# GpSimd's order in a cross attention step: six table entries ahead of the delta's factor

## What is computed

```python
delta = ctx @ Wo.T + bo                       # after softmax attention over ctx_2048, 16 heads
delta = rs * delta
mu, var = mean(delta), mean((delta - mu) ** 2)
delta = (delta - mu) / sqrt(var + EPS_LN) * ln_gamma + ln_beta
x = x + delta
xf = layernorm(x)
scores = softmax(xf @ gate_weight.T)          # 64 experts in 8 groups, best 3 groups, best 6 experts
slot = expert * 192 + position of the token in its expert
```

## Time and profile before

| | us |
|---|---|
| median of three timed runs | 1599.75 (1599.74 to 1600.75) |
| the profiled execution, its own time | 1597.56 |
| its span, first to last instruction | 1595.9 |
| TensorE busy | 1486.6 (93%) |
| VectorE busy | 1139.3 (71%) |
| ScalarE busy | 897.5 (56%) |
| GpSimd busy | 772.4 (48%) |
| cross attention, steps 0 to 15 and what follows the loop | about 325 to 655 |

### The profile page before, as it was taken

The page is one execution under the profiler, slowest core; times in us unless marked ns, Lnnn a source line. Parts: engine busy times, 40 slices in busy tenths (PEclk is TensorE's granted clock), DMA queues, the critical chain, the costliest instruction groups (busy, mean ns, idle before and its releaser), DMA issues.

```text
span 1595.9 us, 30498 instructions
## 1 busy us (share of the span) xinstructions
PE 1486.6 (93%) x10360; PEld 1232.2 (77%) x10360; DVE 1139.3 (71%) x2054; ACT 897.5 (56%) x1769; POOL 772.4 (48%) x957
## 2 busy tenths in 40 slices
PE   6999998999999865499999999999999999999997
PEld 4788886778888754388888888888888888777866
DVE  5677757557888787577777777777777777565656
ACT  4565666644544331187777777777777778412111
POOL 2122234233365556265565555565555564437543
PEclk9999999999999976599999999999999999999999
DMA  6012212222211110598777787777887775437553
GB/s 205 7 55 85 62 54 91 95 71 74 75 66 41 41 54 34 202 365 294 270 266 259 275 289 264 267 267 263 277 289 263 268 262 200 137 119 225 178 177 119
DMA packets 109217, 275.48 MB, mean 173 GB/s; under 512 B 16592, under 2 KB 16592, under 8 KB 109136
## 3 DMA queue, kind: packets, MB, share of 16 engines
q1 hardware_dynamic: 91392, 223.53, 41.0%
q0 software_dynamic: 15360, 50.34, 9.8%
q10 hardware_dynamic: 2384, 0.53, 0.2%
HBM read 232.41 MB, written 41.94 MB: 172 GB/s over the span
## 4 chain that ended last, share of the span: by engine, by line
PE 55%; DVE 2%; DMA 1%; issue 0%; POOL 0%; ACT 0%; SPq 0%; DVEq 0%; POOLq 0%
PE e_gu L2386 18%; PE e_gu L2388 9%; PE e_dn_rest L2414 5%; PE e_tr L49 3%; PE e_dn_main L41 3%; PE e_dn_main L43 3%; PE e_dn_main L42 3%; PE h_gt L41 1%; PE h_gt L43 1%; PE h_gt L42 1%; PE h_up L43 1%; PE h_up L41 1%; PE h_up L42 1%; PE h_dn L41 1%; DVE h_acc L2663 1%; PE h_dn L42 1%
## 5 line engine op out<-in xcount | busy, mean ns | idle before, releaser
L2149 POOL TENSOR_TENSOR e_hid<-e_h_raw,e_hid 128x128 fp32r<-128x128 f32 (+1 forms) x192 | 165.6, 863 | 221.3 <-ACT e_hid L2214 221.3
L2386 PE MATMUL e_gu<-e_xT_hi_lo,e_wg 128*128 128x384 f32 (+1 forms) x768 | 231.5, 357 | 1.6 <-issue 1.6
L2386 PE MATMUL e_gu<-e_xT_hi_lo,e_wu 128*128 128x384 f32 (+1 forms) x768 | 230.4, 355 | 0.0
L2388 PE MATMUL e_gu<-e_xT_hi_lo,e_wu 128*128 128x192 f32 (+1 forms) x768 | 193.3, 252 | 0.0
L2388 PE MATMUL e_gu<-e_xT_hi_lo,e_wg 128*128 128x192 f32 (+1 forms) x768 | 193.1, 251 | 0.0
L2157 POOL TENSOR_TENSOR e_wd<-e_raw_d,e_wd 96x512 fp32r<-96x512 f32 x64 | 131.6, 2056 | 35.8 <-ACT e_wd L2199 35.8
L2386 PEld LDWEIGHTS e_gu<-e_xT_hi_lo,e_wg 128*128 128x128 f32 (+1 forms) x768 | 138.0, 180 | 6.8 <-issue 2.6
L2292 DVE TENSOR_TENSOR e_total<-e_gu,e_low 128x384 f32<-128x384 f32 (+1 forms) x192 | 105.5, 549 | 51.5 <-ACT e_low L2209 51.5
L2388 PEld LDWEIGHTS e_gu<-e_xT_hi_lo,e_wg 128*128 128x128 f32 (+1 forms) x768 | 139.8, 182 | 1.4
L2386 PEld LDWEIGHTS e_gu<-e_xT_hi_lo,e_wu 128*128 128x128 f32 (+1 forms) x768 | 137.9, 180 | 3.8
L2388 PEld LDWEIGHTS e_gu<-e_xT_hi_lo,e_wu 128*128 128x128 f32 (+1 forms) x768 | 139.7, 182 | 0.0
(11 more groups left out here) (341 smaller groups left out, 4049.3 us busy)
## 6 DMA issues: line engine op xcount, KB each, us to landing
e_raw_g<-in_L_ffn_Wg_dram SPq DMA_DIRECT2D x64, 704.0 KB, 4.3
e_raw_u<-in_L_ffn_Wu_dram SPq DMA_DIRECT2D x64, 704.0 KB, 5.7
e_raw_d<-in_L_ffn_Wd_dram SPq DMA_DIRECT2D x64, 512.0 KB, 5.9
y_dram<-e_y_main SPq DMA_DIRECT2D x64, 256.0 KB, 6.2
e_raw_d<-in_L_ffn_Wd_dram SPq DMA_DIRECT2D x64, 192.0 KB, 6.4
y_dram<-e_y_rest SPq DMA_DIRECT2D x64, 128.0 KB, 7.0
s_xr<-in_x_dram SPq DMA_DIRECT2D x16, 256.0 KB, 3.8
x_dram<-s_x SPq DMA_DIRECT2D x16, 256.0 KB, 2.5
```

The costliest lines, as they stand in the source:

```text
L2149: pool.tensor_tensor(hid[b][1][0:n, c, :], h_raw[g.odd][b][0:n, c, 0:P], hid[b][0][0:n, c, :].bitcast(F32), ALU.subtract).then_inc(s_hl, 1)
L2386: pe.matmul(bank[0:n, 0:2 * CAP], w[b][0][:, k, m:m + n], xT[:, :, k, toks], start=k == 0, stop=False)
L2388: ins = pe.matmul(bank[0:n, 0:CAP], w[b][1][:, k, m:m + n], xT[:, 0, k, toks], start=False, stop=k == KC - 1)
```

## The change

In GpSimd's loop the call of `delta_factor(t - 1)` moves behind the table entries. What stands ahead of both, and what follows the loop, is the same; no instruction is added or taken out on any engine.

```diff
                 for m in cross_fresh(t + 1):
                     inv_std(m)
-                if t >= 1:
-                    delta_factor(t - 1)
                 for g in range(NG - 3):
                     for i in range(CROSS_GROUPS[g][1] - CROSS_GROUPS[g][0]):
                         if group_steps(g)[1] + i == t:
                             table_entries(g, i)
+                if t >= 1:
+                    delta_factor(t - 1)
             final_rstd(BATCH - 2)
```

## The result

The median of four timed runs is 1610.97 us (1609.23 to 1613.59), against 1599.74 us of the kernel before on the same chip: a ratio of 1.0065, 95% interval 1.0051 to 1.0079. The change costs 11.2 us. In a second comparison the same kernel came out at 1609.96 us against 1602.59, ratio 1.0054 (1.0035 to 1.0073). So 0.54 to 0.65%; the medians differ by 11.2 and 7.4 us, and the two intervals together reach from 0.35 to 0.79%.

A forecast was written before the change was run, and what follows sets the result against it. TensorE was taken as nearly full in the cross attention, losing time only where made to wait. 11.7 + 0.5 + 0.5 - 1.56 - 1.56, about 9.6, plus 2.4 for the clock: 1597.56 + 12.0 + 2.2 = 1611.8 us, range 1604.5 to 1616.5.

The forecast's parts named there:

- The place of the idle time: GpSimd in step 4: its 6.42 us idle time lies ahead of `inv_std`, and the change puts the entries behind it.
- The lateness, step by step: VectorE's delta waits for the factor behind six entries in steps 5, 7, 8, 9 and 10; 11.7 us late in all.
- No slack between VectorE and TensorE: Steps 5 and 7: VectorE's lateness is carried whole, +2.8 and +1.75 us, inferred from TensorE's waits.
- B: Rival: more slack between VectorE and TensorE, steps 5 and 9 carry half; about +5 to +6, 1605 us; chance 0.12.
- C: Rival: TensorE's queued work rides over VectorE's wait, the path is not reached; 1599 to 1600 us; chance 0.06.
- Steps 10 to 15: Loop's end: steps 10, 11, 13, 15 hold entries free; 12 and 14 lose 0.5 us each; 13 and 15 gain 1.56 each.
- The gain of the final norm: Steps 13 and 15: `final_rstd` no longer stands behind the entries, ScalarE's wait of 1.56 us goes each time.
- The clock: TensorE's new idle stretches in steps 7 and 8: one of two followed by a slow clock stretch, costing 2.4 us.
- Rival D: Faster: TensorE lags VectorE in steps 5 to 9 without waiting, only the `final_rstd` gain remains; 1596.6 us; chance 0.03.

The follow-up runs named there:

- ahead: Against the kernel before: entries directly behind the residual, ahead of `context_lo` and `inv_std`, the factor last; 1598.34 us against 1600.93, -0.18%.
- after: The changed kernel itself, first trace and first timed comparison with the kernel before: 1610.97 us against 1599.74, ratio 1.0065.
- again2: The changed kernel with no edit, third trace; one execution, not timed against the kernel before, stage ends 9.8 us later.
- again: The changed kernel with no edit, second trace and second timed comparison with the kernel before: 1609.96 us against 1602.59, +0.54%.
- step4: Against the kernel before: entries ahead of the factor in step 4 only; +0.19% (0.04 to 0.35).
- late: Against the kernel before: entries ahead of the factor in steps 10 to 15 only; -0.27% (-0.38 to -0.16).
- half: Against the kernel before: three of six entries ahead of the factor, three behind, in all 11 steps; 1598.11 us against 1602.59, -0.21%.
- latemoved: Against the kernel before: entries ahead of the factor in steps 10 to 15 only, VectorE's factor wait behind the delta's first operation; -0.24%.
- early: Against the kernel before: entries ahead of the factor in steps 4 and 6 to 9 only; +0.75% (0.55 to 0.94).
- waitmoved: The changed kernel with VectorE's wait for the factor moved behind the delta's first operation; +0.28% against the kernel before.

## Why the prediction held, point by point

**The place of the idle time.** Right, and it decides the case: ahead and after differ in it alone, -1.6 us against +6.6 to +10.2 in the stage.

**The lateness, step by step.** The chain was forecast at +2.8, +1.75, +3.5, +2.6 and +1.2 for VectorE in steps 5, 7, 8, 9 and 10, 11.7 together after 0.2 of slack. The waits in the trace of after are 2.65, 1.62, 3.09, 2.43 and 1.25, and the table's columns differ by 2.7, 1.5 (over steps 6 and 7), 3.2 (4.3 in again2, behind a slow stretch), 2.2 to 3.5 and 1.2. Two terms were too large. In step 8 I counted the 6.98 us that the entries took in the earlier trace rows, and in their new place they took 6.3 to 6.6. In step 9 the forecast gave the factor's new delay 2.6 us; again, with no slow stretch ahead of it, has 2.2, since VectorE, 7.3 us late at the start of step 8, was 6.9 late by the time of `inv_std` (490.71 us, 478.91 before, counted from step 2). At step 10 again stands at 10.6.

**No slack between VectorE and TensorE.** Right. I had inferred it from waits of 0.41 and 0.66 us at two places; step4 shows that 2.4 to 2.5 of 2.7 us reach step 12 and the end. Rivals B and C fall with it: half of the delays of steps 5 and 9 should have vanished, and 0.2 us of step 5's did.

**Steps 10 to 15.** That steps 10 and 11 hold the entries for nothing was right (late: 0 up to step 11). The lateness in steps 12 and 14 was taken at 0.5 each and is 1.07 and 0.66 in late. The gain of the final norm was forecast at 3.1, 2.1 net. Net it is 1.6 to 2.5 in ahead, half, after and latemoved, where step 13 has a granted clock of 0.78, and 3.0 to 4.0 in late, again2 and again, where it has 0.88 or 0.89. So 2.1 fits the first four, and what the others have above it goes with the clock of the last steps, which the forecast left out. The two were not separated by a run. Early, which has the order of before in these steps, also gets back 0.7 us behind step 10, so a part of each figure is variation.

**The clock.** This is the mis-sized term. I took one slow stretch of nearly 7 us at 2.4 us, after the earlier trace rows. In the steps where TensorE has work waiting, a slow stretch is 3.3 to 3.5 us long and costs 1.6 us where TensorE is on the path and 0.25 where VectorE is. There are one, one and three in three traces. By the trace, then, the clock costs about 1.5, 0.3 and 3 us in steps 7 to 9 of after, again and again2 (estimates from these prices), where 2.4 was forecast. That idle time of 2 to 2.5 us may or may not be followed by one, as the forecast said, stands: 2.49 us ahead of `positions` in step 8 was not in again, 2.51 was in after. But pieces under 2 us, which the forecast left out, can be followed by one as well: again has its slow stretch in step 9, whose idle pieces are 0.86 and 1.08 us. What decides it is open. The statement of the Trainium skill (TensorE: Matmul & The Clock Gate, "What's actually happening") that activity and not a count of instructions sets it agrees with these stretches, since the same instructions ran with and without one; it doesn't size them.

**The sum.** Forecast +12.0 in the stage; the traces give +10.2, +6.6 and +9.8, the two timed comparisons +11.2 and +7.4 to +8.7 (the difference of the medians, and 0.54%). The forecast 1611.8 against 1610.97 is nearer than its parts deserve: the chain was about 1 us too high, the clock of steps 7 to 9 was 0.9 and 2.1 us too high for two traces and 0.6 too low for the third, that of the last steps was left out, and the timed medians carry the variation of the stage's start. That the median is met to 1 us is luck; the direction, the path and the place of the loss are not.

**Rival D** (faster, the final norm's gain alone) was the right mechanism under the wrong condition: it is what late shows, -3.0 us with its clock, once the five steps in which the factor is late are left out.

## What to carry to other kernels

Before filling an engine's idle time, look at which instruction stands at its end: work that is put behind that instruction doesn't fill the gap, it delays everything that follows. An instruction of under a microsecond that another engine waits for at the head of its step should have nothing long queued ahead of it unless the long work ends before its own input comes; work out that one difference for every step, since steps with the same code have different neighbours. And where an order helps in some steps and hurts in others, split it by steps.

## What the runs showed of the hardware that I had not expected

Slow stretches of TensorE's clock (1.2 instead of 2.4 GHz) differ from trace to trace of one and the same kernel (one, one and three in steps 7 to 9), and the same 3.3 us at the lower level cost 1.6 us or 0.25 us according to which engine was behind. VectorE's L1532 took 0.65 us in its usual place, 0.75 directly behind a wait, and 0.93 beside the entries in waitmoved. Contention with GpSimd may be behind these 0.3 us; it isn't shown, since L1532 took 0.65 beside entries too. The prediction looked at VectorE's side alone. GpSimd's side shows more: the first of the six entries of step 7 in the trace of before, beside VectorE's L1599, against 1.00 us for the last:

```profile
463.30 1.78 POOL L1245 TENSOR_SCALAR c_entry<-c_iota_cap,c_posk,c_token 128x192 f16<-128x192 f16 x1
463.33 1.02 DVE L1599 TENSOR_TENSOR a_stage<-c_iota,c_tidf 128x384 f16<-128x384 f32 x2
...
469.28 1.00 POOL L1245 TENSOR_SCALAR c_entry<-c_iota_cap,c_posk,c_token 128x192 f16<-128x192 f16 x1
```

That entry and one of 1.26 us beside L1532 and L1536 make the 6.98 of the earlier trace rows. The Trainium skill (SBUF — State Buffer, "Who interferes with whom") has one of the two blocked for a whole instruction. On VectorE's side that would be up to 1.0 us, and no row here shows that much; on GpSimd's side the 0.78 us are more than one of the two L1599 (0.51) and less than both. The start of the stage varies by 4.5 us between executions of the kernel before.
